# Second recomputed pair in its own buffers, pair 13 in two passes, low parts on GpSimd

## The reference

```python
def gn(v, G=32, eps=1e-5): ...                      # group norm over 2 channels x 56 x 56
def block(x):                                       # x: 32 x 64 x 56 x 56, FP32
    out = conv3x3(x, quantize_weight(w1, 8), b1)
    out = relu(batchnorm(out, gamma1, beta1))       # statistics over all images
    out = conv3x3(out, quantize_weight(w2, 8), b2)
    out = batchnorm(out, gamma2, beta2)
    return relu(out + x)
result = x + block(gn(x))
```

## Time and profile before

| | us |
|---|---|
| median of 3 runs | 526.12 (525.89 to 526.38) |
| the profiled execution | 526.89 |
| its span | 525.1 |

### The profile page before, as it was taken

The page is one execution under the profiler, slowest core; times in us unless marked ns, Lnnn a source line. Parts: engine busy times, 40 slices in busy tenths (PEclk is TensorE's granted clock), DMA queues, the critical chain, the costliest instruction groups (busy, mean ns, idle before and its releaser), DMA issues.

```text
span 525.1 us, 23736 instructions
## 1 busy us (share of the span) xinstructions
PE 494.5 (94%) x11003; PEld 424.4 (81%) x11003; DVE 451.3 (86%) x648; ACT 368.8 (70%) x410; POOL 85.9 (16%) x155
## 2 busy tenths in 40 slices
PE   4999999999999999999999999999997888979994
PEld 2899999999999787899888888898886466567552
DVE  7999989999999966998888898878796989988874
ACT  3899799999999964766655565566622799677472
POOL 2027256666651200000000000000001000000000
PEclk9999999999999999999999999999998999979998
DMA  8934775533333000001343300000056899999997
GB/s 276 362 131 130 257 265 175 196 134 134 131 135 129 10 9 7 2 4 64 136 172 142 128 2 4 4 2 4 2 180 257 324 402 413 428 385 422 382 415 328
DMA packets 23098, 92.99 MB, mean 177 GB/s; under 512 B 8152, under 2 KB 9560, under 8 KB 18776
## 3 DMA queue, kind: packets, MB, share of 16 engines
q1 hardware_dynamic: 22816, 91.19, 45.8%
q10 hardware_dynamic: 184, 0.30, 0.2%
HBM read 58.27 MB, written 32.28 MB: 172 GB/s over the span
## 4 chain that ended last, share of the span: by engine, by line
PE 88%; DVE 5%; issue 2%; ACT 2%; DMA 1%; SPq 1%; DVEq 0%; ACTq 0%
PE conv_ps L1409 71%; PE conv_ps L1531 6%; PE conv_ps L1554 5%; PE conv_ps L1577 4%; DVE slots L1288 1%; DMA slots<-in_x_dram 1%; DVE slots L1294 1%; PE conv_ps L1539 1%; DVE bn_tup L1097 1%; SPq L371 1%; DVE split L1317 0%; ACT split L623 0%; ACT split L818 0%; DVE xa L1310 0%; DMA slots<-slots 0%
## 5 line engine op out<-in xcount | busy, mean ns | idle before, releaser
L1409 PE MATMUL conv_ps<-split,wmat 64*64 64x385 f16 (+3 forms) x9216 | 380.4, 324 | 2.2 <-ACT split L623 1.8
L1409 PEld LDWEIGHTS conv_ps<-split,wmat 64*64 64x64 bf16 x9216 | 345.2, 107 | 33.6 <-issue 3.3
L657 ACT ACTIVATE slots<-conv_ps,par,evac_scale 128x784 f32<-128x784 f32 x124 | 123.7, 998 | 94.0 <-PE conv_ps L1409 92.3
L1097 DVE BATCH_NORM_STATS2 bn_tup<-slots 128x6 f32<-128x392 f32 x164 | 80.8, 554 | 12.8 <-ACT slots L657 12.8
L984 DVE BATCH_NORM_STATS2 small<-slots 128x6 f32<-128x448 f32 x112 | 61.8, 612 | 1.3 <-DMA slots<-in_x_dram 1.3
L1062 DVE TENSOR_TENSOR split<-slots,split 128x3136 f16<-128x3136 f32 (+4 forms) x36 | 57.2, 1606 | 3.9 <-ACT slots L637 0.9
L1064 DVE SCALAR_TENSOR_TENSOR split<-slots,split 128x3248 f16<-128x3248 f32 (+3 forms) x18 | 53.6, 2978 | 2.3
L1040 DVE TENSOR_SCALAR slots<-slots,bn_w 128x3248 f32<-128x3248 f32 (+3 forms) x18 | 30.4, 1687 | 19.7 <-ACT split L613 19.1
L613 ACT ACTIVATE split<-slots,bn_w 128x3248 f16<-128x3248 f32 x14 | 43.2, 3082 | 0.0
L665 ACT ACTIVATE xa<-conv_ps,par,evac_scale 128x784 bf16<-128x784 f32 x40 | 39.7, 994 | 0.0
L1554 PE MATMUL conv_ps<-split,wmat 64*64 64x385 f16 (+3 forms) x576 | 29.5, 346 | 7.1 <-ACT split L818 3.4
(11 more groups left out here) (159 smaller groups left out, 417.4 us busy)
## 6 DMA issues: line engine op xcount, KB each, us to landing
slots<-in_x_dram SPq DMA_DIRECT2D x13, 1568.0 KB, 12.1
slots<-in_x_dram SPq DMA_DIRECT2D x51, 392.0 KB, 5.2
out_dram<-slots SPq DMA_DIRECT2D x7, 1568.0 KB, 7.3
out_dram<-slots SPq DMA_DIRECT2D x10, 784.0 KB, 8.5
y_spill<-slots SPq DMA_DIRECT2D x3, 1624.0 KB, 6.2
slots<-y_spill SPq DMA_DIRECT2D x3, 1624.0 KB, 6.8
xa<-in_x_dram SPq DMA_DIRECT2D x2, 1568.0 KB, 11.5
split<-in_x_dram SPq DMA_DIRECT2D x2, 1568.0 KB, 10.0
```

The costliest lines, as they stand in the source:

```text
L657: nc.scalar.activation(dst, src, ACT.Identity, bias=bias, scale=scale, accum_out=total).then_inc(evacuated[ph], 1)
L1097: ins = nc.vector.bn_stats(bn_tup[:, 2 * (n - first) + s, :], rows[s])
L1409: return nc.tensor.matmul(bank[:, r0:r1, w0:w1], lhs, rows[:, top + r0:top + r1, w0 + kx - 1:w1 + kx - 1], start=n == 0 and part is hi_all ...
```

## The change

The second recomputed pair gets buffers of its own: its high and low parts go into `slots[:, FREE]`, its FP32 input into the slot of pair 4, once pair 4 is stored. In exchange the inputs of pairs 9, 10 and 15 go into the halves of `split`, which the first recomputed pair uses, so load 10 waits for that pair's second convolution and load 9 for its last sum. ScalarE makes the second pair's first piece before the last seed of the first pair. GpSimd makes the first low parts of both recomputed pairs, the second piece in two instructions. Pair 13 goes in two passes, its four VectorE steps between the finishes of 12 and 14, and is stored by halves.

```diff
--- before.py
+++ after.py
@@ -59,13 +59,13 @@
     PAIR3 = [PAIR2[t] for t in ORDER3]
     SLOT3 = [None if u == IN_PSUM or u in AGAIN else SLOT2[ORDER3[RELOADED.get(u, u)]] for u in range(NP)]
     FREE = SLOT2[NP - 1]
-    TWO_PASS = (0, 4, 5, 6, 8, 9, 10)
+    TWO_PASS = (0, 4, 5, 6, 8, 9, 10, 13)
     RING = [u for u in range(NP) if u not in TWO_PASS]
 
 
     CUTS0 = [0, CH, 2 * CH, 4 * CH, 6 * CH, PIX]
     PARTS0 = len(CUTS0) - 1
-    STORES = [PARTS0, 2, 2, 2, 2, 2, 1, 1, 2, 2, 1, 1, 1, 1, 1, 1]
+    STORES = [PARTS0, 2, 2, 2, 2, 2, 1, 1, 2, 2, 1, 1, 1, 2, 1, 1]
     KEPT = SPILL - len(AGAIN)
     STRIP = AREA - PIX
     EARLY = RES * STRIP
@@ -248,6 +248,7 @@
         again_act1 = sem("again_act1")
         again_hi1 = sem("again_hi1")
         again_lo1 = sem("again_lo1")
+        again_rest = sem("again_rest")
         again_conv1 = sem("again_conv1")
         again_hi2 = sem("again_hi2")
         again_act2 = sem("again_act2")
@@ -298,13 +299,13 @@
 
         halves = [split[:, k].rearrange("p h a -> p (h a)").bitcast(F32) for k in range(2)]
         x3 = [ap[:, 0:PIX] for ap in (
-            slots[:, FREE], halves[0], halves[1], slots[:, FREE], slot3(0), slots[:, FREE], slot3(2), xa, slot3(3), slots[:, FREE],
-            slot3(4), slot3(0), slot3(2), xa, slot3(3), slots[:, FREE])]
+            slots[:, FREE], halves[0], halves[1], slots[:, FREE], slot3(0), slots[:, FREE], slot3(2), xa, slot3(3), halves[0],
+            halves[1], slot3(0), slot3(2), xa, slot3(3), halves[0])]
         AGAIN_J = J - 2
         AGAIN_TOP = 2 * RB + 3
-        again1 = [ap.bitcast(F16)[:, 0:2 * PIX].rearrange("p (h m) -> p h m", h=2) for ap in (halves[0], halves[0])]
-        again_fp32 = [ap[:, 0:PIX] for ap in (halves[1], halves[1])]
-        again2 = [ap.bitcast(F16).rearrange("p (h m) -> p h m", h=2) for ap in (halves[1], halves[1])]
+        again1 = [ap.bitcast(F16)[:, 0:2 * PIX].rearrange("p (h m) -> p h m", h=2) for ap in (halves[0], slots[:, FREE])]
+        again_fp32 = [ap[:, 0:PIX] for ap in (halves[1], slot3(4))]
+        again2 = [ap.bitcast(F16).rearrange("p (h m) -> p h m", h=2) for ap in (halves[1], slot3(4))]
         spread_ps = stat_ps[:, 0:C]
         params_ps = stat_ps[:, C:C + 6]
         combined_ps = stat_ps[:, CH + 8:CH + 10]
@@ -487,10 +488,10 @@
             load(11)
             store_half(5, 0)
             store_half(5, 1)
-            wait_out(5)
+            sp.wait_ge(again_conv2, NQ)
+            load(10)
+            sp.wait_ge(skip_added, nth(AGAIN[0], NQ - 1))
             load(9)
-            wait_stored(4)
-            load(10)
             store_whole(6)
             load(12)
             store_whole(7)
@@ -504,8 +505,12 @@
             store_half(9, 1)
             load(15)
             store_whole(10)
-            for u in range(11, NP):
-                store_ring(u)
+            store_ring(11)
+            store_ring(12)
+            store_half(13, 0)
+            store_ring(14)
+            store_half(13, 1)
+            store_ring(15)
             for u in range(NP):
                 wait_stored(u)
 
@@ -585,6 +590,21 @@
                 half = slice(C * h, C * h + C)
                 nc.gpsimd.tensor_scalar(part_diag[half, half], bn_avg[half, half], 2.0 * NP * NQ / GN_SCALE, None,
                                         ALU.mult).then_inc(part_diag_ready, 1)
+
+            def again_low1(r, n):
+                pool.wait_ge(again_act1, 2 * r + n + 1)
+                pool.wait_ge(again_hi1, 2 * r + n + 1)
+                views = [again_parts(again1[r][:, 1], n), again_parts(again_fp32[r], n), again_parts(again1[r][:, 0], n)]
+                if n == 1:
+                    nc.gpsimd.tensor_tensor(*(v[1] for v in views), ALU.subtract).then_inc(again_rest, 1)
+                    pool.wait_ge(again_rest, r + 1)
+                nc.gpsimd.tensor_tensor(*(v[0] for v in views), ALU.subtract).then_inc(again_lo1, 1)
+                pool.wait_ge(again_lo1, 2 * r + n + 1)
+
+            pool.wait_ge(part_diag_ready, 2)
+            for r in range(len(AGAIN)):
+                for n in range(2):
+                    again_low1(r, n)
 
         @block.scalar
         def _(sc):
@@ -800,7 +820,7 @@
 
                 bias, scale = again_affine(r)
                 if r == 1:
-                    sc.wait_ge(again_conv2, NQ)
+                    sc.wait_ge(stored[4], 16 * STORES[4])
                 sc.wait_ge(again_coef, len(AGAIN))
                 sc.wait_ge(x3_loaded[AGAIN[r]], 16)
                 sc.wait_ge(ring_out, nth(2, NQ - 1))
@@ -813,7 +833,7 @@
                 if r == 0:
                     sc.wait_ge(stored[IN_PSUM], 16 * STORES[IN_PSUM])
                 else:
-                    sc.wait_ge(skip_added, nth(AGAIN[0], NQ - 1))
+                    sc.wait_ge(two_out, first_two(5) + 2)
                 for h, xs in zip(again_parts(again1[r][:, 0], n), again_parts(x3[AGAIN[r]], n)):
                     ins = nc.scalar.activation(h, xs, ACT.Identity, bias=bias, scale=scale)
                 ins.then_inc(again_hi1, 1)
@@ -877,11 +897,12 @@
             seed_again(0, 1)
             two_affine(8, 0)
             seed_again(0, 2)
+            make_act1(1, 0)
+            make_hi1(1, 0)
+            seed_again(0, 3)
+            make_act1(1, 1)
+            make_hi1(1, 1)
             two_affine(8, 1)
-            seed_again(0, 3)
-            for n in range(2):
-                make_act1(1, n)
-                make_hi1(1, n)
             two_affine(9, 0)
             make_act2(1, 0)
             two_affine(9, 1)
@@ -892,7 +913,11 @@
             make_act2(1, 3)
             for q in range(NQ):
                 seed_again(1, q)
-            for u in range(12, NP):
+            for k in range(NQ):
+                seed(12, k)
+            two_affine(13, 0)
+            two_affine(13, 1)
+            for u in (14, 15):
                 for k in range(NQ):
                     seed(u, k)
 
@@ -1310,12 +1335,6 @@
                 nc.vector.scalar_tensor_tensor(out=banked(out_of(u), u, k), in0=sums_in(k), scalar=0.0, in1=banked(x3[u], u, k),
                                                op0=ALU.max, op1=ALU.add).then_inc(ring_out, 1)
 
-            def again_low1(r, n):
-                dve.wait_ge(again_act1, 2 * r + n + 1)
-                dve.wait_ge(again_hi1, 2 * r + n + 1)
-                for l, a, h in zip(again_parts(again1[r][:, 1], n), again_parts(again_fp32[r], n), again_parts(again1[r][:, 0], n)):
-                    ins = nc.vector.tensor_tensor(l, a, h, ALU.subtract)
-                ins.then_inc(again_lo1, 1)
 
             def again_low2(r, q):
                 dve.wait_ge(again_hi2, NQ * r + q + 1)
@@ -1338,8 +1357,6 @@
                     finish(u, k)
             for r, (first, second, third) in enumerate(((4, 5, 6), (8, 9, 10))):
                 u = AGAIN[r]
-                again_low1(r, 0)
-                again_low1(r, 1)
                 two_pass(first, 0)
                 two_pass(first, 1)
                 again_low2(r, 0)
@@ -1354,16 +1371,22 @@
                 two_pass(second, 3)
                 finish(u, 0)
                 two_pass(third, 0)
+                two_pass(third, 1)
                 finish(u, 1)
-                two_pass(third, 1)
                 two_pass(third, 2)
                 finish(u, 2)
                 two_pass(third, 3)
                 finish(u, 3)
-            for u in range(12, NP):
+            for u, steps in ((12, (0, 1)), (14, (2, 3)), (15, ())):
                 dve.wait_ge(x3_loaded[u], 16)
-                for k in range(NQ):
-                    finish(u, k)
+                finish(u, 0)
+                finish(u, 1)
+                if steps:
+                    two_pass(13, steps[0])
+                finish(u, 2)
+                finish(u, 3)
+                if steps:
+                    two_pass(13, steps[1])
 
         @block.tensor
         def _(pe):
@@ -1611,7 +1634,7 @@
                     again_round2(r, q)
                     add_parts(r, q - 1)
                 add_parts(r, 3)
-            for u in range(12, NP):
+            for u in (12, 14, 15):
                 add_sums(u)
 
 
```

## The result

The changed kernel takes 530.25 us (529.99 to 530.54) against 526.0 for the kernel before, measured beside it: a ratio of 1.0092, with a 95% interval of 1.0072 to 1.0112. That is 0.9% slower, 4 to 5 us where 1.25 was forecast, and above the range of 525.0 to 529.4. Measured again in a later series the ratio was 1.0076 (1.0049 to 1.0103). The profiled execution took 530.43 us, 3.54 more than the profiled one of the kernel before. One execution of the whole case, of the kernel called *the last seed first*, took 1320 us in the slow state, and is in none of the ratios.

What follows compares the result with a forecast made beforehand. The DMA queue was taken to bound the last stage: 2.7 us lost near 457, less 0.95 at the end and 0.5 from old gaps, gave +1.25 us on 526.12, so 527.4 us; range 525.0 to 529.4.

Steps and rivals of the forecast that it cites:

- What bounds: Last stage: DMA queue, not TensorE, sets the end; only 3.4 us of idle DMA time before the change.
- Low parts on GpSimd: First recomputed pair: GpSimd takes 4.3 us for 1904 columns, so TensorE starts the low part 1.8 us late.
- Load 10's issue: SyncE issues load 10 near 458.5 us, after the first recomputed pair's second convolution.
- Own buffers and pair 13: Second pair starts without half clock, saving TensorE 2.5 us; tail 1.4 to 2 us shorter; last finish at 515.6.
- The price of the dry stretch: Near 457 us the queue runs dry before the gated loads; every later landing comes 2.7 us later.
- the 1.35: Time in us that an idle queue adds to a transfer's own service, taken from pair 15's store.
- The gain at the end and the 0.5 us: Last store gains 0.95 us from a queue never dry; 0.5 us more returns from gaps at 496-500 and 514-516.
- Rival D: Second low-part piece: GpSimd and VectorE slow each other, the piece taking 6.0 us; 528.3 us or more; 11%.
- Rival C: TensorE falls to half clock in its new wait, 428.2 to 430.55 us; 529.1 to 530.8 us; 12%.
- A: Rival: transfers are no bound, so the last finish 3.9 us earlier gives 522.2 us; 7%.
- B: Rival: GpSimd needs only 2.13 us, the queue hardly runs dry near 457; 524.1 to 526.1 us; 20%.

Runs made afterwards that it cites:

- the last seed first: Changed kernel with the first recomputed pair's last seed moved ahead of the second pair's first piece on ScalarE; ratio 1.0055 to the kernel before.
- the repeated kernel: The changed kernel measured once more with nothing altered, on the chip of the follow-up runs; ratio 1.0076 to the kernel before.

## Why the prediction was wrong

The mechanism was the one forecast: the gated loads let the queue run dry, every later landing is late by that, and the computation that ends 3.9 us earlier finds the queue full. The size of one term was wrong, the dry stretch. By its steps:

- *What bounds.* Right: full shares to 524, and the last store 12.6 us in the queue (9 to 11 us had been expected from the last finish to the end, it is 13.0). Seven slices before the last stood at 9, not eight; nothing hangs on it.
- *Low parts on GpSimd.* 4.3 us were taken, it was 3.81; the wait on TensorE was 2.00 for 2.35. The estimate of 4.2 from the figure of the Trainium skill's page GPSIMD Engine Reference (section Elementwise: side-by-side cycle accounting) is 0.1 nearer.
- *Load 10's issue.* 458.5 forecast, 458.37 measured.
- *Own buffers and pair 13.* No half clock near 461 and the last finish at 515.59, forecast 515.6. Right, and worth nothing.
- *The price of the dry stretch.* This is the step that failed, the term of the sum that was mis-sized: 2.7 us, when the second load landed 469.7 - 464.7 = 5.0 us late. Put right, the reading of the kernel before leaves the 2.7 as it was: with the landing at 464.7 both loads there were served in 3.7 to 3.8 us, so 458.5 + 1.35 + 3.75 + 3.75 = 467.4 would have been forecast. Two parts of it were wrong. A load from an idle queue took 6.4 us (6.3 in the trace of the repeated kernel), not 1.35 + 3.75 = 5.1, as the 1.35 came from a store: 1.3 us. And load 9 was put right behind load 10, when it waits for a sum whose seed stands behind 3.84 us of the second pair's first piece on ScalarE; it went out 3.2 us after load 10 and landed 4.9 us after it instead of 3.75, with one transfer alone in the queue, which moved 119 and 320 GB/s: 1.2 us. Against these stands an issue 0.1 us earlier than forecast. The prediction's part on own buffers had that late seed, 0.6 us, and charged it to TensorE, not to the load. The kernel with the seed first gives 1.1 us of it back.
- *The gain at the end and the 0.5 us.* Both about right. Pair 14's store, the last but one, landed at 520.0 before; all but the last store of the changed kernel has landed at 512.1 + 12.4 = 524.5, 4.5 us later. So of the 5.0 some 0.5 came back where the old gaps were. The last store then lands at 515.6 + 12.6 = 528.2 against 519.5 + 5.1 = 524.6 (the prediction had 524.7), 3.6 us later: 0.9 more came back because it no longer started from an idle queue, and 0.95 had been reckoned.

So the sum closes for the two profiled executions, from which its terms are taken: 5.0 - 0.5 - 0.9 = 3.6 us, and they are 3.54 us apart. By the two ratios the kernels are 4.0 to 4.8 us apart; the rest is of the size by which executions of one kernel differ (528.3 to 531.7 us for the repeated one), and stays unassigned.

Rival D had the place right and the victim wrong. In the changed kernel GpSimd's large subtraction took 3.81 us both times, beside VectorE or not; it was VectorE that stood, 5.33 and 3.49 us for passes of 1.8. Where VectorE's pass had begun first, GpSimd waited as well: in the kernel with the seed first its 1904 columns, begun at 460.96 during a pass from 460.48 on, took 5.01 us. That is the conflict of the Trainium skill's page GPSIMD Engine Reference (section Specifications), between GpSimd and VectorE instructions with two inputs in SBUF. Rival C did not come: the granted clock was 1.00 from 428 to 434 us, with the 2.00 us of waiting inside. A was ruled out by the store's 12.6 us, B by the 2.00.

By the kernels' differences the loss splits so: gating load 10, together with the order on ScalarE that makes the last seed late, costs 2.1 to 2.9 us (1.0037 against 1.0076 and 1.0092); GpSimd's low parts cost 1.6 (1.0037 against 1.0007); the rest is nothing that can be told. No kernel undid the gate alone, so its own price is not shown; the seed's order is some 1.1 us of it by the kernel with the seed first. Still open is what part of GpSimd's 1.6 us is TensorE's wait and what VectorE's hold-up; both delay stores and loads, and the kernel with only the second pair on GpSimd did not part them.

## What to carry to other kernels

Where the DMA share stands near 1 for a whole stage, as here, suspect the queue as the bound even if the chain names TensorE, and test it by taking one transfer out; then ask of every edit what it does to the time at which transfers are issued, above all whether a load that was free to go now waits for a computation, and whether the transfers in front of it cover the wait. Price such a dry stretch by when the queue is deep again, not by when the first load goes out: what else stands behind the same wait, and in which order its releasers are made, counts too. Computation that ends earlier gives back only the gaps of the queue: here 5.7 us earlier gave nothing that could be told. The bound is not one-sided: computation that ended later, as with GpSimd alone in the kernel before, was paid for.

## What the runs showed of the hardware

- GpSimd's two-input subtraction ran at 2.0 to 2.1 ns a column (1904 columns in 3.81 us, 1008 in 2.12), FP32 and FP16 in and FP16 out; VectorE took 2.13 us for the 1904.
- Beside it, VectorE's two-input passes in SBUF did not slow in proportion but stood for it: 1.79 us became 5.33, with a small GpSimd instruction (224 columns) at 1.86 instead of 0.61 next to them. The one that began later waited: GpSimd's 1904 columns took 5.01 us behind a pass that had begun 0.5 us before them.
- A load of 1568 KB from an idle queue landed after 6.4 us, a store of the same size after 5.1; in a full queue either takes its turn of 3.7 to 3.8 us.
